# A graph layer's edge stage on one core: VectorE's rank work first in its turn, and its offset chain in two parts at other slots

## The chip, the cores and the metric

The kernel runs on one core of a Trainium2 chip. The metric is the device time in microseconds of one execution. TensorE (PE in the profile) does the matmuls, VectorE (DVE) and ScalarE (ACT) the elementwise work, GpSimd (POOL) issues the indirect transfers, and SyncE's queue (SP) the plain ones.

## What is computed

The reference is one message-passing layer with 6250 nodes and 206250 edges (100000 random pairs in both directions and a loop at each node, sorted by their destination), with a residual and a layer norm around it:

```python
row, col = src, dst
msg = concat([x[col], edge_attr], axis=1)          # 206250 x 128
h = relu(msg @ W1a.T + b1a) @ W1b.T + b1b          # 206250 x 64
sums = segment_sum(h, row, 6250); counts = segment_sum(1, row, 6250)
agg = sums / max(counts, 1)
z = relu(concat([x, agg]) @ W2a.T + b2a) @ W2b.T + b2b
out = concat([z, x]) @ Wr.T + br
y = layernorm(x + out)
```

Edges arrive sorted by `dst`, but the sums go by `src`. So each edge's result has to be moved to the place of its source node.

## The kernel before

The 206250 edges are cut into 403 quads of 512 edges. The edge stage treats two quads in each turn `m` of the table `TURNS`: quads 2m and 2m+1 enter, and the two quads before them leave. The order of every engine's work within a turn is written out by hand, one loop over `TURNS` for each engine, and the engines meet at semaphores only.

For a quad, `hidden` (L482) is the first linear layer, in float32, with a one-hot window of destination nodes that VectorE builds in `onehot` (L828). ScalarE applies the relu (L681). `message` (L492) is the second layer for two quads, into MS. ScalarE copies MS to Z (`copy_x`, L688), and beside it a class column (L692). VectorE's `rest` (L834) and `low` (L841) subtract from MS what Z holds in bfloat16, so that Z carries the float32 value in three bfloat16 parts. `permute` (L505) sorts the 512 edges of a quad by class of source node (a class is 128 nodes), with the one-hot matrices M that VectorE builds in `places` (L850) from the positions `pos`, into PA and PBk. ScalarE evicts these into stg (L703), and POOL scatters stg to the DRAM tensor `region`, at the rows that `dest` names (L1109). When all are scattered, the gather stage reads the runs of each class back, sums them by node and does the node layers.

Where an edge goes is worked out on the way. This is the rank work, in slots `i`, two for each turn:

- `rank(i)` on TensorE: class counts of a later quad into CK (L539), the rank of each edge among its class (L565, L567, into RK), and the destinations of quad i+4 (L577). `rank(2m)` stands between `hidden(2m+1)` and `permute(2m-2)`, `rank(2m+1)` at the turn's end.
- `ranks(i)` on VectorE: `positions(i+5)`, a reduction of RK to pos (L856), which must be done before TensorE's `rank(i+1)` writes RK again; in every second turn `destinations` (L926, L929); and at some slots the offset chain.

A block has 31 quads, and there are 13. When the classes of a block are counted, the offset chain works out where its edges begin in each class. It has four steps, each behind a small matmul of `rank`: `chain_copy` (L860, L864), `chain_counts` (L868 to L874), `chain_places` (L877 to L899) and `chain_steps` (L902 to L907). For block b they stand at the slots 31b-10, 31b-9, 31b-8 and 31b-7. `chain_places` copies the offsets out of RK, then does ten instructions on 50x62 values up to `dd`, which the matmul of `rank(31b-7)` reads (L560). These instructions wait for each other through the semaphore s_ch1. `stair` (L916) makes the matrix S for the destinations from them.

`classes` (L818) compares the classes of two quads `LEAD` ahead, and `index` (L797 to L809) prepares a block of indices for it, at the start of the turn. The ring OC of the comparisons holds 40 quads.

VectorE's turn before:

```python
for m in TURNS:
    # index, if a block begins at 2m+LEAD
    rest(m - 1); low(m - 1); places(2 * m - 2, 0)
    ranks(2 * m - 1)
    places(2 * m - 2, 1)
    onehot(m + 1)
    ranks(2 * m)
    stair(m + 3)
    places(2 * m - 1, 0); places(2 * m - 1, 1)
    classes(m + LEAD // 2)
```

`rest(m-1)` waits for s_x, ScalarE's class column. TensorE's `permute(2m-2, 0)` waits for s_l (`low`) and s_M (the second `places`), and `message(m)` for s_r (`rest`), since it writes MS again.

Of the kernel before, what the change touches and what calls it, by code (L numbers as in the profile page):

```python
# [38 lines left out]
LEAD = 42  # L39
# [26 lines left out]
def program(nc, xt, dstr, srcc, dstc, ea, wpk, cst, pos3, out):  # L66
# [9 lines left out]
    with ctx:  # L76
# [302 lines left out]
        def pe_ranks(i):  # L379
            return (0 <= i + 40 < NQ or 0 <= i + 5 < NQ or 0 <= i + 4 < NQ or block_at(i, 9) is not None  # L380
                    or block_at(i, 8) is not None or block_at(i, 7) is not None or i in (TABLES + 1, TABLES + 2))

        def dve_ranks(i):
            return (0 <= i + 5 < NQ or block_at(i, 10) is not None or block_at(i, 9) is not None
                    or block_at(i, 8) is not None or block_at(i, 7) is not None
                    or (0 <= i + 4 < NQ and ((i + 4) % 4 == 3 or i + 4 == NQ - 1))
                    or i in (TABLES + 1, TABLES + 2))
# [17 lines left out]
        with nc.Fori(0, trips) as _k:  # L405
            with nc.Block() as block:
# [60 lines left out]
                def _(e):  # L467
# [43 lines left out]
                    def rank(i):  # L511
# [4 lines left out]
                        b = block_at(i - 1, 10)  # L516
                        if b is not None:
                            e.wait_ge(s_ch1, LINKS * b + 2)
                        b = block_at(i - 1, 9)
                        if b is not None:  # L520
                            e.wait_ge(s_ch1, LINKS * b + 3)
                        b = block_at(i - 1, 8)
# [12 lines left out]
                        q = i + 40  # L535
# [6 lines left out]
                        b = block_at(i, 9)  # L542
# [7 lines left out]
                        b = block_at(i, 8)  # L550
# [218 lines left out]
                def _(e):  # L769
# [106 lines left out]
                    def chain_places(b):  # L876
# [3 lines left out]
                            "p (g c) -> p g c", g=2)[:, :, None, :].to_broadcast([BQ, 2, 2, CL])))  # L880
                        link(e.tensor_tensor_scan(run_in[:, :], oneg[:, :], kc[:, :], 0.0, ALU.mult, ALU.add))
# [90 lines left out]
                    def ranks(i):  # L972
                        if not dve_ranks(i):
                            return
                        e.wait_ge(s_rk, pe_count[i])
                        if 0 <= i + 5 < NQ:
                            positions(i + 5)
                        if block_at(i, 10) is not None:
                            chain_copy(block_at(i, 10))
                        if block_at(i, 9) is not None:  # L980
                            chain_counts(block_at(i, 9))
                        if block_at(i, 8) is not None:
                            chain_places(block_at(i, 8))
                        if block_at(i, 7) is not None:
                            chain_steps(block_at(i, 7))
                        if 0 <= i + 4 < NQ and ((i + 4) % 4 == 3 or i + 4 == NQ - 1):
                            destinations(i + 4)
                        if i == TABLES + 1:
                            tables()
                        if i == TABLES + 2:  # L990
                            next_pass()
# [10 lines left out]
                    for m in TURNS:  # L1002
                        for i in (2 * m + LEAD, 2 * m + LEAD + 1):
                            if i % BQ == 0 and i < NQ:
                                index(i // BQ)
                        if 0 <= m - 1 < NP:
                            rest(m - 1)
                            low(m - 1)
                            places(2 * m - 2, 0)
                        ranks(2 * m - 1)  # L1010
                        if 0 <= m - 1 < NP:
                            places(2 * m - 2, 1)
# [5 lines left out]
                        if 0 <= 2 * m - 1 < NQ:  # L1018
                            places(2 * m - 1, 0)
                            places(2 * m - 1, 1)  # L1020
                        if 0 <= m + LEAD // 2 < NP:
                            classes(m + LEAD // 2)
# [188 lines left out]
```

## Time and profile before

| | before |
|---|---|
| median of 3 runs | 1813.52 us (1808.44 to 1814.13) |
| the profiled execution | 1807.23 us, its span 1805.6 us |
| TensorE, matmuls | 1639.8 us busy, 91% |
| TensorE, weight loads | 1341.6 us, 74% |
| VectorE | 1404.7 us, 78% |
| ScalarE | 905.8 us, 50% |
| GpSimd | 1044.8 us, 58% |
| granted TensorE clock, mean | 0.963 of full |

The span is from the first to the last instruction. Up to some 55 us the kernel prepares its tables, then the edge stage runs to about 1475 us, and the rest is the gather stage. Busy shares are averages over all of these. Weight loads run beside matmuls. The number behind an instruction's name in a timeline is how many neighbouring instructions of the same kind were put in one row, and the time in brackets is how long the engine was idle before it, and for what.

### The profile page before, as it was taken

To read this page: it belongs to the slowest core of one execution; us is meant where nothing else is said; L and a number is where in the kernel's file an instruction comes from. 1 tells how busy PE (TensorE), PEld (TensorE's weight loads), DVE (VectorE), ACT (ScalarE), POOL (GpSimd) and SP (SyncE) were. 2 spreads that over 40 slices of the span, in tenths; PEclk is the share of its full clock that TensorE was granted. 3 is DMA by queue.
4 is the path that set the end of the run, shared out by engine and by line. 5 is a ranking of instruction groups with operands and counts; after the bars stand their busy time and mean duration, and the time that the engine had idled before them with its cause. 6 is when DMAs were issued, how large, how long until landed. Compare 5 with 4: busy or idle time off the path is not lost.

```text
span 1805.6 us, 40992 instructions
## 1 busy us (share of the span) xinstructions
PE 1639.8 (91%) x13455; PEld 1341.6 (74%) x13455; DVE 1404.7 (78%) x3936; ACT 905.8 (50%) x1733; POOL 1044.8 (58%) x880
## 2 busy tenths in 40 slices
PE   7899999999999999999999999999999957888787
PEld 6677777777777777777777777777777747777676
DVE  5788888888888888888888888888887745666665
ACT  2365656566565665656666565665656640011101
POOL 2376767677675776757667576775766751112210
PEclk9899999999999999999999999999999988889898
DMA  7355555555554555545555455554555658999994
GB/s 226 87 149 141 155 142 155 146 149 155 141 151 129 157 154 142 152 131 156 153 143 154 127 156 143 154 154 127 155 146 154 167 164 351 354 361 362 339 376 165
DMA packets 127789, 326.02 MB, mean 181 GB/s; under 512 B 35617, under 2 KB 68419, under 8 KB 121310
## 3 DMA queue, kind: packets, MB, share of 16 engines
q0 software_dynamic: 46080, 217.15, 37.3%
q1 hardware_dynamic: 80902, 104.09, 22.7%
q10 hardware_dynamic: 600, 2.16, 0.4%
q8 instruction: 112, 1.84, 0.4%
q14 instruction: 95, 0.78, 0.1%
HBM read 203.87 MB, written 119.40 MB: 179 GB/s over the span
## 4 chain that ended last, share of the span: by engine, by line
PE 77%; DMA 9%; DVE 7%; issue 5%; ACT 1%; POOL 0%; POOLq 0%; DVEq 0%; ACTq 0%
PE MS L492 19%; PE HH L482 19%; PE PA L505 13%; PE PBk L505 12%; DMA gbuf<-region,idx 8%; PE PA L618 5%; PE CK L539 2%; PE RK L565 2%; PE RK L567 2%; DVE OH L1032 1%; DVE M L850 1%; PE RK L577 1%; DVE Z L834 1%; DVE pos L856 0%; POOL region L1109 0%
## 5 line engine op out<-in xcount | busy, mean ns | idle before, releaser
L1109 POOL DMA_INDIRECT region<-stg,dest x806 | 968.1, 1201 | 465.9 <-ACT stg L703 283.9
L482 PE MATMUL HH<-eab,pw 128*128 128x512 f32 x806 | 438.0, 626 | 1.6 <-ACT hT L681 1.6
L850 DVE TENSOR_SCALAR M<-pos_of,pos 128x384 bf16<-128x384 int16 x1612 | 427.1, 314 | 0.1
L492 PE MATMUL MS<-W,hT 128*128 128x64 f32 x3224 | 392.7, 276 | 0.0
L492 PEld LDWEIGHTS MS<-W,hT 128*128 128x128 f32 x3224 | 382.7, 195 | 0.0
L703 ACT ACTIVATE stg<-PA 120x585 bf16<-120x585 f32 x403 | 266.4, 661 | 153.6 <-PE PA L505 153.5
L681 ACT ACTIVATE hT<-HH 128x512 f32<-128x512 f32 x403 | 240.6, 597 | 198.1 <-PE HH L482 198.1
L505 PEld LDWEIGHTS PA<-Z,M 128*128 128x128 bf16 x2418 | 215.1, 97 | 166.1 <-issue 158.0
L505 PE MATMUL PA<-Z,M 128*128 128x195 bf16 x2418 | 290.1, 255 | 38.6 <-issue 34.9
L834 DVE TENSOR_TENSOR Z<-MS,Z 128x512 f32<-128x512 f32 x202 | 139.2, 689 | 196.3 <-ACT Z L692 196.3
L505 PE MATMUL PBk<-Z,M 128*128 128x195 bf16 x2418 | 288.1, 254 | 0.0
L618 PE MATMUL PA<-gbuf,OH 128*128 128x195 bf16 x2058 | 209.9, 267 | 67.7 <-DVE OH L1032 67.6
L703 ACT ACTIVATE stg<-PBk 120x585 bf16<-120x585 f32 x403 | 265.0, 658 | 0.1
L618 PEld LDWEIGHTS PA<-gbuf,OH 128*128 128x128 bf16 x2058 | 197.7, 106 | 85.0 <-issue 80.8
L688 ACT ACTIVATE Z<-MS 128x512 f32<-128x512 f32 x202 | 120.4, 596 | 226.9 <-PE MS L492 226.9
L1032 DVE TENSOR_TENSOR OH<-laneb,ids 128x2688 bf16<-128x2688 bf16 x98 | 148.2, 1553 | 101.0 <-ACT ids L757 101.0
L505 PEld LDWEIGHTS PBk<-Z,M 128*128 128x128 bf16 x2418 | 224.5, 97 | 0.1
L1125 POOL DMA_INDIRECT gbuf<-region,idx x49 | 59.4, 1213 | 235.1 <-PE PA L618 231.4
L828 DVE TENSOR_SCALAR eab<-kb,C 64x1024 f32<-64x1024 bf16 x202 | 160.1, 793 | 6.4
L539 PEld LDWEIGHTS CK<-OC,ind 128*128 128x128 bf16 x403 | 50.5, 126 | 143.7 <-DVE pos L856 122.9
L856 DVE TENSOR_REDUCE pos<-RK 128x4 f32<-128x200 f32 x403 | 146.1, 363 | 14.1 <-PE RK L577 7.9
L841 DVE TENSOR_TENSOR Z<-Z 128x512 bf16<-128x512 f32 x202 | 150.4, 745 | 6.9
(183 smaller groups left out, 1309.3 us busy)
## 6 DMA issues: line engine op xcount, KB each, us to landing
eab<-in_ea SPq DMA_DIRECT2D x201, 256.0 KB
kb<-keyd SPq DMA_DIRECT2D x201, 128.0 KB
pw<-ptab SPq DMA_DIRECT2D x403, 32.0 KB
region<-stg,dest POOLq DMA_INDIRECT x806
ptab<-OH SPq DMA_DIRECT2D x10, 256.0 KB, 5.0
eab<-in_xt SPq DMA_DIRECT2D x12, 130.0 KB
eab<-in_xt SPq DMA_DIRECT2D x12, 128.0 KB, 8.9
out_y<-kb SPq DMA_DIRECT2D x12, 128.0 KB, 3.6
```

What stands on the lines that cost most here:

```text
L482: e.matmul(HH[:, :], pw[:, q % 4, :], eab[:, c % NB, at_q:at_q + GE], start=True, stop=True).then_inc(s_h, 1)
L492: last = e.matmul(MS[:, o:o + D], hT[:, q % 2, 128 * j:128 * j + 128], W[:, W_1B:W_1B + D], start=True, stop=True)
L505: last = e.matmul(P[:, 256 * j:256 * j + 3 * PART].rearrange("p (k f) -> p k f", k=3), M[:, q % 2, 2 * h + t, j, :], Zb[:, q // 2 % 2, :, ...
L618: last = e.matmul(o, OH[:, c % 2, k, j, :], gb[:, c % 3, ROW * k + 3 * PART * j:ROW * k + 3 * PART * (j + 1)], start=k == 0 and j == 0, st ...
L681: e.activation(hT[:, q % 2, :], HH[:, :], ACT.Relu).then_inc(s_relu, 1)
L703: e.activation(stb[:, g % NS, 0:9 * PART].rearrange("p (j f) -> p j f", j=R), P[0:KC, 0:768].rearrange("p (j f) -> p j f", j=R)[:, :, 0:3 ...
L828: e.tensor_scalar(eab[64:128, c % NB, 0:w], kb[64:128, c % NB, 0:w], C[64:128, C_P64:C_P64 + 1], None, ALU.is_equal).then_inc(s_oh, 1)
L834: e.tensor_tensor(Z[:, m % 2, 1, 0:n, 0:D], MS[:, 0:n * D].rearrange("p (j f) -> p j f", f=D), Zb[:, m % 2, 0, 0:n, 1:2 * D:2], ALU.subtra ...
L841: e.tensor_tensor(Zb[:, m % 2, 2, 0:n, 1:2 * D:2], Z[:, m % 2, 1, 0:n, 0:D], Zb[:, m % 2, 1, 0:n, 1:2 * D:2], ALU.subtract).then_inc(s_l, 1)
L850: last = e.tensor_scalar(M[:, q % 2, t, :, :], pos_of[:, :, :], pos[:, q % 16, t:t + 1], None, ALU.is_equal)
L1032: e.tensor_tensor(OH[:, c % 2, TR * h:TR * h + TR, :, :].rearrange("p k j (n u) -> p (k j) n u", u=2), lane2[:, None, :, :].to_broadcast([ ...
L1109: e.indirect_dma_start(region, bass.IndirectOffsetOnAxis(ap=dest[:, g:g + 1], axis=0), stw[:, g % NS, :], None).then_inc(s_sc[g % NS], 16)
```

## The change

`LEAD` goes from 42 to 44, and with it the counting of classes from slot i+40 to i+42. `chain_copy`, `chain_counts` and the first part of `chain_places` move to the slots 31b-12, 31b-11 and 31b-10, `chain_steps` stays at 31b-7. The ten instructions of `chain_places` after the copies become `chain_runs`, which stands behind the turn's last `places`. In VectorE's turn `ranks(2m-1)` comes first, then both halves of `places(2m-2)`, then `rest` and `low`. `index` moves from the turn's start to a place ahead of `classes`. Within `ranks`, `destinations` comes ahead of the chain.

```diff
-LEAD = 42
+LEAD = 44
...
         def pe_ranks(i):
-            return (0 <= i + 40 < NQ or 0 <= i + 5 < NQ or 0 <= i + 4 < NQ or block_at(i, 9) is not None
-                    or block_at(i, 8) is not None or block_at(i, 7) is not None or i in (TABLES + 1, TABLES + 2))
+            return (0 <= i + 42 < NQ or 0 <= i + 5 < NQ or 0 <= i + 4 < NQ or block_at(i, 11) is not None
+                    or block_at(i, 10) is not None or block_at(i, 7) is not None or i in (TABLES + 1, TABLES + 2))
...
-                        b = block_at(i - 1, 8)
+                        b = block_at(i - 1, 10)
                         if b is not None:
                             e.wait_ge(s_ch1, LINKS * b + 7)
...
-                        q = i + 40
+                        q = i + 42
                         if 0 <= q < NQ:
                             e.wait_ge(s_oc, q // 2 + 1)
...
-                        b = block_at(i, 8)
+                        b = block_at(i, 10)
                         if b is not None:
                             e.wait_ge(s_ch1, LINKS * b + 6)
...
+
+                    def chain_runs(b):
+                        after_link()
                         link(e.tensor_tensor_scan(run_in[:, :], oneg[:, :], kc[:, :], 0.0, ALU.mult, ALU.add))
...
+                        if 0 <= i + 4 < NQ and ((i + 4) % 4 == 3 or i + 4 == NQ - 1):
+                            destinations(i + 4)
+                        if block_at(i, 12) is not None:
+                            chain_copy(block_at(i, 12))
+                        if block_at(i, 11) is not None:
+                            chain_counts(block_at(i, 11))
                         if block_at(i, 10) is not None:
-                            chain_copy(block_at(i, 10))
-                        if block_at(i, 9) is not None:
-                            chain_counts(block_at(i, 9))
-                        if block_at(i, 8) is not None:
-                            chain_places(block_at(i, 8))
+                            chain_places(block_at(i, 10))
                         if block_at(i, 7) is not None:
                             chain_steps(block_at(i, 7))
-                        if 0 <= i + 4 < NQ and ((i + 4) % 4 == 3 or i + 4 == NQ - 1):
-                            destinations(i + 4)
...
                     for m in TURNS:
-                        for i in (2 * m + LEAD, 2 * m + LEAD + 1):
-                            if i % BQ == 0 and i < NQ:
-                                index(i // BQ)
+                        ranks(2 * m - 1)
                         if 0 <= m - 1 < NP:
+                            places(2 * m - 2, 0)
+                            places(2 * m - 2, 1)
                             rest(m - 1)
                             low(m - 1)
-                            places(2 * m - 2, 0)
-                        ranks(2 * m - 1)
-                        if 0 <= m - 1 < NP:
-                            places(2 * m - 2, 1)
                         if 0 <= m + 1 < NP:
                             onehot(m + 1)
                         ranks(2 * m)
...
+                        for i in (2 * m - 1, 2 * m):
+                            if block_at(i, 10) is not None:
+                                chain_runs(block_at(i, 10))
+                        for i in (2 * m + LEAD, 2 * m + LEAD + 1):
+                            if i % BQ == 0 and i < NQ:
+                                index(i // BQ)
                         if 0 <= m + LEAD // 2 < NP:
                             classes(m + LEAD // 2)
```

The first place is VectorE in a turn with destinations, in the middle of the edge stage. Z is what `rest` and `low` write, M the one-hot matrices, eab the one-hot window, S `stair`'s matrix and OC the class comparison. Before:

```order
L834 TENSOR_TENSOR Z<-MS,Z 128x8x64
L841 TENSOR_TENSOR Z<-Z 128x8x64
L850 TENSOR_SCALAR M<-pos_of,pos 128x384 x2
L856 TENSOR_REDUCE pos<-RK 128x4
L926 TENSOR_REDUCE dsum<-RK 120x8
L929 TENSOR_SCALAR dest<-dsum,C 120x8
L850 TENSOR_SCALAR M<-pos_of,pos 128x384 x2
L828 TENSOR_SCALAR eab<-kb,C 64x1024
```

Of the change:

```order
L856 TENSOR_REDUCE pos<-RK 128x4
L929 TENSOR_REDUCE dsum<-RK 120x8
L932 TENSOR_SCALAR dest<-dsum,C 120x8
L850 TENSOR_SCALAR M<-pos_of,pos 128x384 x4
L834 TENSOR_TENSOR Z<-MS,Z 128x8x64
L841 TENSOR_TENSOR Z<-Z 128x8x64
L828 TENSOR_SCALAR eab<-kb,C 64x1024
```

The instructions up to the one-hot window are the same; the reduction of RK and the destinations went from the middle to the front, and `rest` and `low` from the front to the end.

The second place is VectorE in the chain of block 5, from the last instructions of the part that makes `dd` to the steps. Before:

```order
L897 TENSOR_TENSOR dd<-dd,use 50x62
L899 TENSOR_TENSOR dd<-dd,C 50x62
L926 TENSOR_REDUCE dsum<-RK 120x8
L929 TENSOR_SCALAR dest<-dsum,C 120x8
L850 TENSOR_SCALAR M<-pos_of,pos 128x384 x2
L828 TENSOR_SCALAR eab<-kb,C 64x1024
L856 TENSOR_REDUCE pos<-RK 128x4
L902 COPY Dz<-RK 50x62
L904 TENSOR_TENSOR Dz<-Dz 50x62
```

Of the change:

```order
L900 TENSOR_TENSOR dd<-dd,use 50x62
L902 TENSOR_TENSOR dd<-dd,C 50x62
L818 TENSOR_TENSOR OC<-clsb,cls 128x400
L856 TENSOR_REDUCE pos<-RK 128x4
L929 TENSOR_REDUCE dsum<-RK 120x8
L932 TENSOR_SCALAR dest<-dsum,C 120x8
L850 TENSOR_SCALAR M<-pos_of,pos 128x384 x4
L834 TENSOR_TENSOR Z<-MS,Z 128x8x64
L841 TENSOR_TENSOR Z<-Z 128x8x64
L828 TENSOR_SCALAR eab<-kb,C 64x1024
L856 TENSOR_REDUCE pos<-RK 128x4
L905 COPY Dz<-RK 50x62
```

The part that makes `dd` now stands at the end of the turn before, behind that turn's M builds, and a whole first half of a turn lies between it and the steps.

## Rows read from the trace of the kernel before

**Rows 1.** Waits: engine line <- what it waited for: us in all, times, longest

```profile
DVE Z L834 <- ACT Z L692: 196.3, 185, 2.3
...
PE CK L539 <- DVE dsum L926: 13.1, 11, 2.3
...
PE RK L560 <- DVE dd L899: 11.9, 10, 1.8
```

**Rows 2.** One line's instructions: L692, once in each turn of the edge stage

```profile
L692 ACT ACTIVATE Z<-lid x202: 201/208/211, 63.6 to 1468.9; 128x8 f32<-128x8 f32 x101
```

**Rows 3.** Timeline, a plain turn: start, duration in us, engine, line, out<-in, count

```profile
807.12 0.20 PE L577 MATMUL RK<-Dz,S 128*128 128x3 bf16 x2
...
807.56 0.21 ACT L692 ACTIVATE Z<-lid 128x8 f32<-128x8 f32 x1
807.80 0.69 DVE L834 TENSOR_TENSOR Z<-MS,Z 128x512 f32<-128x512 f32 x1 [1.62 <-ACT Z L692]
...
808.53 0.75 DVE L841 TENSOR_TENSOR Z<-Z 128x512 bf16<-128x512 f32 x1
...
809.62 0.36 DVE L856 TENSOR_REDUCE pos<-RK 128x4 f32<-128x200 f32 x1
...
809.89 0.55 DVE L850 TENSOR_SCALAR M<-pos_of,pos 128x384 bf16<-128x384 int16 x2
...
810.37 0.20 PE L577 MATMUL RK<-Dz,S 128*128 128x3 bf16 x2
810.47 0.85 DVE L828 TENSOR_SCALAR eab<-kb,C 64x1024 f32<-64x1024 bf16 x1
...
810.54 0.72 PE L505 MATMUL PA<-Z,M 128*128 128x195 bf16 x6
...
812.08 0.99 DVE L850 TENSOR_SCALAR M<-pos_of,pos 128x384 bf16<-128x384 int16 x4
...
812.99 0.35 DVE L818 TENSOR_TENSOR OC<-clsb,cls 128x400 bf16<-128x400 bf16 x1
...
813.65 0.20 PE L577 MATMUL RK<-Dz,S 128*128 128x3 bf16 x2
```

**Rows 4.** Timeline, the turn after it, which has destinations

```profile
816.41 0.17 DVE L926 TENSOR_REDUCE dsum<-RK 120x8 f32<-120x24 f32 x1
...
816.76 0.65 DVE L850 TENSOR_SCALAR M<-pos_of,pos 128x384 bf16<-128x384 int16 x2
...
817.51 0.72 PE L505 MATMUL PA<-Z,M 128*128 128x195 bf16 x6 [0.38 <-issue]
...
820.62 0.20 PE L577 MATMUL RK<-Dz,S 128*128 128x3 bf16 x2
```

**Rows 5.** Timeline, a permute for which VectorE was not late

```profile
803.96 0.20 PE L577 MATMUL RK<-Dz,S 128*128 128x3 bf16 x2
...
804.01 0.72 PE L505 MATMUL PA<-Z,M 128*128 128x195 bf16 x6
```

**Rows 6.** Timeline, places and runs in the chain of block 5

```profile
572.26 0.20 DVE L877 COPY offs<-RK 50x62 f32<-50x62 f32 x1
...
572.85 0.27 DVE L881 TENSOR_TENSOR_SCAN run_in<-oneg,kc 50x62 f32<-50x62 f32 x1
...
574.91 0.17 DVE L926 TENSOR_REDUCE dsum<-RK 120x8 f32<-120x24 f32 x1
```

**Rows 7.** Timeline, the first instruction of index and the one that follows index

```profile
554.66 0.27 DVE L797 TENSOR_TENSOR kd<-dc,baseB 128x124 f32<-128x124 int32 x1
...
555.96 0.68 DVE L834 TENSOR_TENSOR Z<-MS,Z 128x512 f32<-128x512 f32 x1
```

**Rows 8.** Busy time by stretch: us, PE, PEld, DVE, ACT, POOL busy, clock, DMA

```profile
577.00:584.00 7.00, 7.00 (x34) 5.63 (x32) 4.69 (x16) 2.27 (x5) 2.22 (x2) 0.51 0.22 63
```

**Rows 9.** POOL's scatters: the costliest groups, then one of the timeline

```profile
L1109 POOL DMA_INDIRECT region<-stg,dest x806 | 968.1, 1201 | 465.9 <-ACT stg L703 283.9
...
812.49 1.73 POOL L1109 DMA_INDIRECT region<-stg,dest  x1 [0.30 <-issue]
```

More of the change, by code:

```diff
@@ L379, in pe_ranks @@
         def pe_ranks(i):
-            return (0 <= i + 40 < NQ or 0 <= i + 5 < NQ or 0 <= i + 4 < NQ or block_at(i, 9) is not None
-                    or block_at(i, 8) is not None or block_at(i, 7) is not None or i in (TABLES + 1, TABLES + 2))
+            return (0 <= i + 42 < NQ or 0 <= i + 5 < NQ or 0 <= i + 4 < NQ or block_at(i, 11) is not None
+                    or block_at(i, 10) is not None or block_at(i, 7) is not None or i in (TABLES + 1, TABLES + 2))
         def dve_ranks(i):
-            return (0 <= i + 5 < NQ or block_at(i, 10) is not None or block_at(i, 9) is not None
-                    or block_at(i, 8) is not None or block_at(i, 7) is not None
+            return (0 <= i + 5 < NQ or block_at(i, 12) is not None or block_at(i, 11) is not None
+                    or block_at(i, 10) is not None or block_at(i, 7) is not None
                     or (0 <= i + 4 < NQ and ((i + 4) % 4 == 3 or i + 4 == NQ - 1))
@@ L515, in rank @@
                             e.wait_ge(s_dst, i + 5)
-                        b = block_at(i - 1, 10)
+                        b = block_at(i - 1, 12)
                         if b is not None:
                             e.wait_ge(s_ch1, LINKS * b + 2)
-                        b = block_at(i - 1, 9)
+                        b = block_at(i - 1, 11)
                         if b is not None:
                             e.wait_ge(s_ch1, LINKS * b + 3)
-                        b = block_at(i - 1, 8)
+                        b = block_at(i - 1, 10)
                         if b is not None:
@@ L541, in rank @@
                                             start=k == 0, stop=k == BQ - 1)
-                        b = block_at(i, 9)
+                        b = block_at(i, 11)
                         if b is not None:
```

## The prediction

> **What bounds the kernel now.** The stretch to read is the edge stage, in which every turn treats two quads. I took the views in this order: waits, one instruction that runs once a turn, the timeline of one plain turn, one with destinations, and the turns of one offset chain.
>
> The waits show VectorE idle 196 us for ScalarE's copy of the class column (L692), and TensorE idle for two links of the rank work, at most 2.3 us at a time but only 25 us in all [rows 1]. L692 runs 202 times between 63.6 and 1468.9 us [rows 2]: 1405.3 us for 201 turns, 6.99 us a turn. About 340 us of the span lie outside (prologue and gather); the change leaves them alone.
>
> In a plain turn [rows 3] I take the end of TensorE's second rank step as T (807.12 + 0.20 = 807.32; the next is 6.53 us later). VectorE has been idle, ScalarE ends L692 at 807.77, VectorE begins `rest` at 807.80, T + 0.48, and from there works without a gap through `low`, two M builds, pos and two more M builds to 810.44, 2.64 us. TensorE's `permute(2m-2)` starts at 810.54. It needs all of that, so it starts at T + 0.48 + 2.64 + 0.10 = T + 3.22, and 3.31 us later the turn is over. The loop is closed: message, ScalarE's copy, VectorE, permute, message. That TensorE would have been ready earlier is seen where VectorE was not late: there permute starts 0.05 us after the last pair of rank matmuls has started [rows 5], here 0.17 [rows 3]. So a turn without this wait is 0.12 shorter, 6.41 us, with permute at T + 3.10.
>
> In every second turn `destinations` sits between pos and the last two M builds [rows 4]: dsum 816.41, the M builds only at 816.76 and 0.65 long, permute at 817.51, T + 3.66. This turn is 6.97 us (813.65 to 820.62).
>
> 100 plain turns of 6.53 and 101 of 6.97 make 1357 us. The other 48 us belong to the 12 chains of blocks 1 to 12, 4.0 us each (block 0's runs before the first edge).
>
> **The change part by part.** (1) *Rank work first.* `ranks(2m-1)` no longer waits behind `rest` for ScalarE; it waits only for TensorE's own rank step. I let it start 0.03 us after that step, as `rest` starts behind L692 [rows 3]: T + 0.03. What permute needs is unchanged in amount. By [rows 3], pos to M is 0.27 (809.62 to 809.89), four M builds take 0.91 up to the next start (812.08 to 812.99), `rest` 0.73, `low` 0.74: 2.65 us. `low` ends at T + 2.68. L692 (T + 0.45) has been done for a microsecond when `rest` comes (T + 1.2), so that wait is gone. Permute could start at T + 2.78; TensorE itself is ready at T + 3.10, so a plain turn is 6.41. With destinations, VectorE has 0.36 to 0.46 more (0.35 of start-to-start in [rows 4], and 0.1 of the longer M builds): permute at T + 3.15 to 3.25, so 6.46 to 6.56; I take 6.51. Saved: 100 x 0.12 + 101 x 0.46 = 58.5 us.
>
> The second half of VectorE's turn (one-hot, pos, S, four M builds, classes) is unchanged, 810.47 to 813.27, 2.8 us. VectorE is then free at T + 5.5 in a plain turn and near T + 5.95 with destinations: 0.9 and 0.55 us of slack before the next T.
>
> (2) *The chain.* Its instructions are the same. I take places as 0.59 (572.26 to 572.85), the ten instructions of `chain_runs` as 2.06 (572.85 to 574.91) [rows 6]; copy is two, counts four and steps three instructions of the size of the 0.20 row or somewhat more, with waits between: an estimate of 0.6, 0.8 and 0.7. Before, in odd blocks, all of places and runs stood between pos and M in the first half: that is TensorE's longest wait, 2.3 us [rows 1]. Now runs come after the M builds, and steps three slots later instead of one, so no TensorE matmul waits for runs directly. But 2.06 us does not fit into the slack: VectorE enters the next turn late, and what permute needs is late with it. Odd block: 2.06 less the slack of 0.9 or 0.55 is 1.2 or 1.5, and where it is 1.5 the next turn is plain and swallows 0.3: permute is 1.2 late. Even block: places and runs fall into the same second half, 2.65 less 0.9, or less 0.55 and 0.3: 1.8. The smaller pieces delay permute wherever they stand in a first half, by their length, or by 0.3 less in a plain turn. `index` (1.30 us [rows 7]), now at the turn's end, leaves VectorE 0.4 to 0.7 late into the turn of copy. So, for an odd block: runs 1.2, index and copy 1.0, places 0.5, the chain's own matmuls on TensorE 0.4 (0.3 each, one or two not hidden), 3.1 in all. For an even one: runs 1.8, index 0.4, counts 0.7, steps 0.55, matmuls 0.6, 4.05 in all. The average is 3.6 against 4.0: 5 us saved over 12 blocks.
>
> (3) *LEAD 44, slots 12, 11, 10.* One more turn in the ramp, with one class comparison of 0.35 us (L818 in [rows 3]) and 0.3 us of matmul. The waits of `classes` for the OC ring now name rank(2m), which VectorE has waited for already: nothing. Scatters get their destinations earlier: nothing, POOL isn't short of them. At the end of the stage POOL, which now has less slack a turn, may finish later than the last eviction. For ramp and end together I charge 2 us.
>
> Sum: 58.5 + 5 - 2 = 61.5, about 62 us. The profiled execution took 1807.2 us, so 1745; it is 6.3 us under the median of 1813.5, and I carry the gain over to that: **1751 us**.
>
> The ends of the unknown terms: the plain turn may stay at 6.53 (another wait at the same place), 12 us less; the turn with destinations may be 6.46 or 6.56, 5 us either way; lateness may cost 2.5 or 5 us a block, 13 less or 17 more. Together 1738 to 1765, rarely all at once.
>
> **The rivals.** *The half clock.* From 577 to 584 us the granted clock was 0.51 [rows 8], the lower of 1.2 and 2.4 GHz, right after the end of block 5's runs (574.91, [rows 6]), for which TensorE had stood idle. A stretch of some 7 us at half clock costs about 3.4. Not every odd block has such a dip, and the even blocks, whose longest wait was 1.8 us [rows 1], have none. Of my waits behind runs, the odd blocks' 1.2 to 1.5 us is under these and the even blocks' 1.8 to 2.1 between the two. If every even block falls, 6 x 3.4 = 20 us: 1771; if all twelve, 41: 1790. Against it: the waits are shorter than those that did it, and four dips of before may vanish, which are part of the 48 us above. The Trainium skill ("TensorE: Matmul & The Clock Gate", What's actually happening) has TensorE's clock set by how busy it has been; by that, a denser stage would have fewer dips, not more. The trace agrees in that its dips follow idle.
>
> *POOL becomes the bound.* A scatter takes 1.20 us on average, 0.30 between two [rows 9]: 6.0 us a turn, and the new turn is 6.46. The scatter that began at 812.49 under four M builds in a row took 1.73. Now there are two such rows of four in a turn, so a second scatter may be stretched. If two of four are (2 x 1.30 + 2 x 2.03 = 6.66 us), the pace is that of my sum, chain included (1345 us for 202 turns): no loss. At a mean of 1.70 from start to start, 6.80 a turn, the stage takes 1374 and the kernel 1782. *Its bad end is my case on the other side:* three of four stretched, 7.39 us a turn, 1493 us, 88 more than now, 1901. It decides from 1.74 us between starts (1405.3 / 202 / 4). Against it: in the turns with destinations the first row of four starts 0.4 later, beside another scatter or none. The Trainium skill ("SBUF — State Buffer", Who interferes with whom) says that a VectorE instruction in a two-port mode and GpSimd block each other wholly on a shared port; the 1.73 row fits that.
>
> *VectorE is the bound.* In 15.5 turns it has 15.5 x 5.76 + 6.0 = 95 us of 100 that TensorE now needs. If its instructions are 8% longer than I take them, through POOL, the stage loses another 25 us: 1776.
>
> *The change does not remove the wait.* If something keeps `ranks(2m-1)` waiting for a message-time event, nothing changes: 1813. TensorE's rank step ends 0.45 before L692 does [rows 3], so I see nothing that would.
>
> **How the numbers follow.** Forecast 0.66 (1738 to 1765); half clock 0.13 (1766 to 1790); POOL at its mild end or VectorE 0.13 (1766 to 1790); no gain 0.03; POOL slower than now 0.05. The range 1736 to 1788 holds the forecast and most of the next two. A measurement of this kernel can tell 0.3%, some 5 us, from no change. Faster 0.92, same 0.03, slower 0.05.
>
> **What would show it.** Right: L692's 202 runs span about 1343 us; plain turns near 6.41, the others near 6.51; no VectorE wait for L692 in most turns, but one for the last rank matmul L577; permute a tenth of a microsecond behind `low` in the turns with destinations; a permute 1.2 to 2 us late in the turn after each `chain_runs`. Wrong: plain turns of 6.53; POOL without idle time in the middle of the stage, or scatters of 1.7 us twice a turn; a granted clock of 0.5 after every block.

## The result

The change made the kernel faster by 3.5%. The chain of experiments behind it shows that most of the gain is the wait that the prediction named, and that the offset chain's part works mainly through TensorE's clock.

| | before | after |
|---|---|---|
| median of 4 runs each | 1811.54 us | 1748.69 us |
| range | 1808.44 to 1814.13 | 1745.73 to 1750.30 |
| ratio, 95% interval | | 0.9652, 0.9629 to 0.9674 |
| profiled execution | 1807.23 us, span 1805.6 | 1750.30 us, span 1748.6 |
| from first to last L692 | 1405.3 us | 1346.2 us |

1751 was predicted, with 1736 to 1788 as the range.

### The profile page after: what moved, and what is told of

Read it like the earlier page. It is cut to its first block, busy times and chain, and to the rows that moved or that the text cites. A ratio compares the mean times of both kernels' runs of the same rounds, so it can differ in the third digit from the quotient of the medians.

```text
span 1748.6 us, 40992 instructions
## 1 busy us (share of the span) xinstructions
PE 1611.3 (92%) x13455; PEld 1335.1 (76%) x13455; DVE 1411.4 (81%) x3936; ACT 906.4 (52%) x1733; POOL 1005.7 (58%) x880
## 4 chain that ended last, share of the span: by engine, by line
PE 61%; DVE 22%; DMA 9%; issue 4%; POOL 2%; ACT 1%; DVEq 0%; POOLq 0%; ACTq 0%
PE MS L492 17%; PE HH L482 12%; PE PA L505 10%; PE PBk L505 9%; DMA gbuf<-region,idx 9%; DVE M L850 6%; PE PA L618 6%; DVE Z L841 4%; DVE Z L834 3%; DVE pos L856 2%; PE RK L565 2%; PE RK L567 1%; PE CK L539 1%; POOL region L1114 1%; DVE OH L1037 1%
## 5 line engine op out<-in xcount | busy, mean ns | idle before, releaser
L1114 POOL DMA_INDIRECT region<-stg,dest x806 | 924.0, 1146 | 453.3 <-ACT stg L703 271.4
L850 DVE TENSOR_SCALAR M<-pos_of,pos 128x384 bf16<-128x384 int16 x1612 | 413.8, 315 | 0.9 <-PE PBk L505 0.4
L492 PE MATMUL MS<-W,hT 128*128 128x64 f32 x3224 | 388.1, 274 | 0.0
L492 PEld LDWEIGHTS MS<-W,hT 128*128 128x128 f32 x3224 | 378.2, 193 | 0.0
L703 ACT ACTIVATE stg<-PA 120x585 bf16<-120x585 f32 x403 | 266.6, 662 | 107.3 <-PE PA L505 106.0
L703 ACT ACTIVATE stg<-PBk 120x585 bf16<-120x585 f32 x403 | 265.2, 658 | 0.6 <-PE PBk L505 0.3
L856 DVE TENSOR_REDUCE pos<-RK 128x4 f32<-128x200 f32 x403 | 147.4, 366 | 141.2 <-PE RK L577 133.6
L1130 POOL DMA_INDIRECT gbuf<-region,idx x49 | 63.1, 1287 | 229.1 <-PE PA L618 225.3
L757 ACT ACTIVATE ids<-gbuf 128x84 bf16<-128x84 bf16 x49 | 13.7, 280 | 279.5 <-DMA gbuf<-region,idx 279.5
L828 DVE TENSOR_SCALAR eab<-kb,C 64x1024 f32<-64x1024 bf16 x202 | 151.9, 752 | 6.5
```

The lines of the kernel that those rows point to most:

```text
L492: last = e.matmul(MS[:, o:o + D], hT[:, q % 2, 128 * j:128 * j + 128], W[:, W_1B:W_1B + D], start=True, stop=True)
L703: e.activation(stb[:, g % NS, 0:9 * PART].rearrange("p (j f) -> p j f", j=R), P[0:KC, 0:768].rearrange("p (j f) -> p j f", j=R)[:, :, 0:3 ...
L850: last = e.tensor_scalar(M[:, q % 2, t, :, :], pos_of[:, :, :], pos[:, q % 16, t:t + 1], None, ALU.is_equal)
L856: e.tensor_reduce(pos[:, q % 16, :], RK[:, 0:4 * CL].rearrange("p (t c) -> p t c", t=4), AX.X, ALU.max).then_inc(s_dst, 1)
L1114: e.indirect_dma_start(region, bass.IndirectOffsetOnAxis(ap=dest[:, g:g + 1], axis=0), stw[:, g % NS, :], None).then_inc(s_sc[g % NS], 16)
```

## The profile after

Lines of the page of the kernel after: busy time, the granted clock, and three of its groups. Three lines were added to `chain_runs` and two to the loop, so L1109 is now L1114, L926 is L929 and L916 is L919; up to L880 the numbers stand.

```profile
PE 1611.3 (92%) x13455; PEld 1335.1 (76%) x13455; DVE 1411.4 (81%) x3936; ACT 906.4 (52%) x1733; POOL 1005.7 (58%) x880
...
PEclk9699999999999999999999999999999979899898
...
L1114 POOL DMA_INDIRECT region<-stg,dest x806 | 924.0, 1146 | 453.3 <-ACT stg L703 271.4
...
L856 DVE TENSOR_REDUCE pos<-RK 128x4 f32<-128x200 f32 x403 | 147.4, 366 | 141.2 <-PE RK L577 133.6
...
L834 DVE TENSOR_TENSOR Z<-MS,Z 128x512 f32<-128x512 f32 x202 | 137.0, 678 | 2.3 <-ACT Z L692 2.1
```

VectorE's wait for ScalarE's class column has gone from 196.3 us to 2.1 [rows 1]. It now waits for TensorE's rank step instead, 133.6 us at L856: that is the slack it has left. The scatters did not get longer, 1146 ns against 1201 [rows 9], and POOL is still idle for evictions.

The waits of the kernel after, TensorE's and its weight loads' (us in all, times, longest):

```profile
PEld PA L505 <- DVE Z L841: 40.2, 79, 2.1
PE PA L505 <- DVE Z L841: 28.3, 38, 2.0
```

This is `permute` waiting for `low`: the turns with destinations and those behind the chain. Now the timeline, a plain turn and the one with destinations behind it (start, duration in us, engine, line, out<-in, count, wait before):

```profile
806.35 0.20 PE L577 MATMUL RK<-Dz,S 128*128 128x3 bf16 x2
806.58 0.37 DVE L856 TENSOR_REDUCE pos<-RK 128x4 f32<-128x200 f32 x1 [0.57 <-PE RK L577]
806.78 0.21 ACT L692 ACTIVATE Z<-lid 128x8 f32<-128x8 f32 x1
806.86 1.00 DVE L850 TENSOR_SCALAR M<-pos_of,pos 128x384 bf16<-128x384 int16 x4
...
807.78 0.69 DVE L834 TENSOR_TENSOR Z<-MS,Z 128x512 f32<-128x512 f32 x1
...
808.50 0.74 DVE L841 TENSOR_TENSOR Z<-Z 128x512 bf16<-128x512 f32 x1
...
809.59 0.20 PE L577 MATMUL RK<-Dz,S 128*128 128x3 bf16 x2
809.65 0.72 PE L505 MATMUL PA<-Z,M 128*128 128x195 bf16 x6
...
812.76 0.20 PE L577 MATMUL RK<-Dz,S 128*128 128x3 bf16 x2
812.99 0.37 DVE L856 TENSOR_REDUCE pos<-RK 128x4 f32<-128x200 f32 x1 [0.91 <-PE RK L577]
...
813.62 1.19 DVE L850 TENSOR_SCALAR M<-pos_of,pos 128x384 bf16<-128x384 int16 x4
...
815.45 0.79 DVE L841 TENSOR_TENSOR Z<-Z 128x512 bf16<-128x512 f32 x1
815.99 0.20 PE L577 MATMUL RK<-Dz,S 128*128 128x3 bf16 x2
...
816.29 0.48 PEld L505 LDWEIGHTS PA<-Z,M 128*128 128x128 bf16 x6 [0.20 <-DVE Z L841]
...
819.42 0.20 PE L577 MATMUL RK<-Dz,S 128*128 128x3 bf16 x2
```

The plain turn is 6.41 us from rank step to rank step (806.35 to 812.76). `low` ends at 809.24, `permute` starts at 809.65, right behind the rank matmuls: VectorE is 0.4 us early, and TensorE has hardly a gap left. The turn with destinations is 6.66 (812.76 to 819.42). There `low` ends at 816.24 and `permute` starts 0.05 behind it. The turns with destinations alternate between 6.43 and 6.66; in the longer ones four M builds take 1.15 to 1.19 us instead of 1.00, and `low` 0.79 instead of 0.74.

The traces of before, after and of seven of the experiments were cut up in the same way, by the starts of L692. The base is the mean turn outside the chains. The excess is what the turns of a chain take above the base, summed over the blocks 1 to 12 (all in us). Where the edges of a chain are drawn moves these sums by about 1 us; the expectations have 43.6 for the change by other edges. The excess with the wait put back holds a stretch at half clock in block 4, which took 7.5 us where block 8 took 3.1.

| kernel | plain turn | with destinations | chain excess | turn 0 | L692, first to last |
|---|---|---|---|---|---|
| before | 6.52 | 6.97 | 50.4 | 6.55 | 1405.3 |
| after | 6.41 | 6.55 | 44.3 | 9.30 | 1346.2 |
| order alone | 6.41 | 6.56 | 62.5 | 9.20 | 1365.3 |
| chain alone | 6.52 | 6.97 | 34.7 | 6.56 | 1389.6 |
| with the wait put back | 6.67 | 6.88 | 36.8 | 7.49 | 1399.0 |
| runs in one piece | 6.41 | 6.56 | 73.1 | 7.49 | 1373.8 |
| destinations late | 6.41 | 6.43 | 45.4 | 7.48 | 1338.0 |
| runs in halves | 6.41 | 6.56 | 31.4 | 6.29 | 1331.3 |
| both of these | 6.41 | 6.44 | 34.9 | 9.30 | 1331.8 |

## Experiments on a chip that withholds the gain

The first four kernels were timed on another chip. There the kernel before took 1884.38 us (25 runs, 1871.83 to 1902.27), 4% more than on the first, so these four are compared with that alone.

**The change again.** No edit.

> The change itself once more, beside the pieces below. Theory (the loop through ScalarE's class column was what a turn cost): plain turns 6.41 us, turns with destinations 6.4 to 6.7, about 1749 us. It also shows whether the long half-clock stretch at the start of the edge stage (to 72.7 us; before it ended at 61.7) comes with the change or differs from run to run: if it comes with the change, the first L692 begins near 66 us and the second some 9.3 us later again.

Measured: 1899.39 us, ratio 1.0069 (1.0027 to 1.0112). The gain isn't there.

**The order alone.** The kernel before with this edit:

```diff
                     for m in TURNS:
...
+                        ranks(2 * m - 1)
                         if 0 <= m - 1 < NP:
+                            places(2 * m - 2, 0)
+                            places(2 * m - 2, 1)
                             rest(m - 1)
                             low(m - 1)
-                            places(2 * m - 2, 0)
-                        ranks(2 * m - 1)
-                        if 0 <= m - 1 < NP:
-                            places(2 * m - 2, 1)
```

> The kernel before with VectorE's turn order of the change alone; LEAD 42, the chain whole and at its old slots, destinations behind the chain in ranks. Theory (turn order carries the gain): plain turns 6.41, turns with destinations 6.55, the chains 4 to 5 us a block since all of places and runs stands before the M builds or in one second half; 1302 + 54 us for the 201 turns, about 1760 us in all, with some half-clock dips behind the odd blocks. Rival (the chain's split and new slots carry it): plain turns 6.53, about 1800.

Measured: 1919.29 us, 1.018 (1.0108 to 1.0252).

**The chain alone.** The change with the old order of VectorE's turn put back.

> The change with VectorE's old turn order (rest, low, half of the M builds, ranks, the other half); LEAD 44, split chain, new slots, index late, destinations first in ranks. Theory: plain turns stay 6.53 and turns with destinations 6.97; the runs then have some 1.05 us of VectorE's idle time before rest, so a block costs about 2.6 us instead of 4.0, and the dips behind the odd blocks go: about 1797 us. Rival (the split carries the gain): 1760.

Measured: 1874.76 us, 0.9967 (0.9932 to 1.0002).

**The change with the wait put back.**

```diff
                     for m in TURNS:
+                        if 0 <= m - 1 < NP:
+                            e.wait_ge(s_x, m)
                         ranks(2 * m - 1)
```

> The change with one wait more: VectorE waits for ScalarE's class column (s_x) at the head of the turn, ahead of ranks, as rest did before; same order otherwise. Theory (the wait's place, not the order of the instructions, is what the loop costs): plain turns 6.54, turns with destinations 6.97, chains 2.6 us a block: about 1795 us. Rival (the order of rank work ahead of TensorE's rank step matters by itself): 1749 to 1760.

Measured: 1870.76 us, 0.9928 (0.9892 to 0.9964): here the kernel with the wait that the change removed is *faster* than the change without it (1899.39).

As times, all four expectations were wrong. As ratios, the chain alone (0.992 said) and the wait put back (0.991 said) are near, and the two kernels with the new order and no wait are 4 to 5% off. The waits of the change on this chip show what is different (engine line <- releaser: us in all, times, longest):

```profile
DVE pos L856 <- remote: 136.1, 51, 5.2
ACT Z L688 <- remote: 119.1, 50, 3.0
```

There are no such rows in the trace of after. A stretch of the timeline shows one of them:

```profile
1001.03 1.91 PE L492 MATMUL MS<-W,hT 128*128 128x64 f32 x16
...
1002.25 0.66 ACT L703 ACTIVATE stg<-PBk 120x585 bf16<-120x585 f32 x1 [0.90 <-PE PBk L505]
...
1003.04 0.20 PE L577 MATMUL RK<-Dz,S 128*128 128x3 bf16 x2
...
1005.19 0.60 ACT L688 ACTIVATE Z<-MS 128x512 f32<-128x512 f32 x1 [2.28 <-remote]
1005.25 0.37 DVE L856 TENSOR_REDUCE pos<-RK 128x4 f32<-128x200 f32 x1 [2.84 <-remote]
```

and the row of that stretch in the busy times (PE, PEld, DVE, ACT, POOL busy, granted clock, share of the DMA engines, GB/s):

```profile
1001.00:1005.00 4.00, 4.00 (x37) 3.43 (x35) 1.42 (x6) 1.01 (x2) 3.02 (x3) 1.00 0.79 211
```

The message's record ends at 1002.94. ScalarE's copy of it, which waits for TensorE alone, starts at 1005.19. By the same records the copy starts 0.04 us behind the message in all 202 turns of the trace of after, and of before; on this chip it starts over a quarter of a microsecond later than that in 84 of 202, by up to 3 us. ScalarE and VectorE are let go at the same time. So TensorE's results came late there, at a granted clock that the profile gives as 1.00 (the ends of matmuls in a profile are modelled, and here that shows). Summed over the 202 copies the lateness follows the kernels' times. It is not spread evenly: in the change 121 of the 135 us fall on every second copy, the one that ends a plain turn, and so it is in the other three (125 of 153, 71 of 77, 41 of 52).

| on that chip | copies of the message late by, in all | over 1 us late | L692, first to last |
|---|---|---|---|
| order alone | 153 us | 63 | 1516.1 us |
| the change | 135 | 55 | 1495.9 |
| chain alone | 77 | 15 | 1471.7 |
| with the wait put back | 52 | 17 | 1459.6 |

I had two readings: TensorE's results come late (A), or the evictions wait for scatters to land, since stg has 8 buffers, two turns' worth, and ScalarE also waited 40.3 us at L703 for something unnamed (the ring). The second set was to tell them apart and, if it met a chip like the first, to settle the shares.

## Experiments on chips like the first

The second set of four ran on a chip where the kernel before took 1805.83 us (13 runs), the third where it took 1812.57 (13 runs). In their eight traces none of the 1616 copies of the message starts more than 0.05 us behind it.

**The order alone** (same edit).

> The kernel before with only VectorE's order changed (ranks, one-hots, add, low), the offset chain left at its old slots. It took 1919 us on a chip where the kernel before took 1884. Theory A (the gain is real where TensorE's results reach the other engines as soon as its records end, and that chip withheld them): if the kernel before takes about 1811 us here, this one takes 1752 to 1765 us and the wait of the add for ScalarE's column (196 us before) is gone; if the kernel before takes about 1884 us here, this one takes 1905 to 1930 and the copy of the message starts over 0.3 us behind the record of its matmuls in a third or more of the turns. Rival (the order alone loses on any chip, and the chain's new slots are needed for the gain): about 1.01 to 1.02 of the kernel before on either.

Measured: 1766.07 us, 0.9744 (0.9701 to 0.9787). So the order gains on this chip, 40 us, where the whole change brought 56 in the same set (the kernel with 12 buffers, below), and the rival that the order loses on any chip is out. What held the results back on the other chip this run can't tell, as it has no late copies. The order's chain excess is 62.5 us, 12 more than before. Busy time by stretch at block 5, two rows, and the timeline between them:

```profile
562.00:569.00 7.00, 5.00 (x37) 3.14 (x35) 6.56 (x27) 3.06 (x6) 3.79 (x4) 1.00 0.52 134
569.00:577.00 8.00, 7.69 (x39) 6.34 (x40) 5.79 (x19) 2.29 (x5) 2.35 (x2) 0.57 0.31 97
```

```profile
564.17 0.27 DVE L881 TENSOR_TENSOR_SCAN run_in<-oneg,kc 50x62 f32<-50x62 f32 x1
...
566.66 0.25 PE L539 MATMUL CK<-OC,ind 128*128 128x200 bf16 x1 [0.45 <-DVE dsum L926]
...
569.31 0.72 PE L505 MATMUL PA<-Z,M 128*128 128x195 bf16 x6 [1.86 <-DVE Z L841]
```

The run part of the chain (564.17 to 566.24) stands in the rank work, M, `rest` and `low` come after it, and `permute` waits 1.86 us, in a turn that had a gap of 0.45 already. TensorE's granted clock then falls from full speed (2.4 GHz) to its lower level (1.2 GHz, half) until about 577. That is so at all six odd blocks, behind waits of a permute of 1.47 to 1.86 us; in the kernel before it was four of six.

**The wait put back** (same edit).

> The change with one wait added: VectorE waits for ScalarE's column before the rank work of each turn's first slot, as the order before made it do. It took 1871 us where the kernel before took 1884. Theory A: where the kernel before takes about 1811 us, this one loses nearly all that the change gained: 1785 to 1805 us. Rival (the wait costs nothing, something else in the change gains): 1745 to 1755 us. On a chip where the kernel before takes 1884 us: 1860 to 1880 again by both.

Measured: 1803.78 us, 0.9977 (0.995 to 1.0004). One wait takes back 54 us of the change. (Its plain turn, 6.67, is longer than the 6.52 of before, so this is not exactly what the old wait cost.) Its waits have the row of before in a new place:

```profile
DVE pos L856 <- ACT Z L692: 174.3, 169, 3.2
```

**Destinations late and runs in halves together** (both edits below).

> The change with the destinations behind the 16-bit write of the message (TensorE waits for them at its second matmul group) and the runs of the chain in two halves, one slot pair earlier. Theory A: on a chip where the kernel before takes 1811 us the turns with destinations come down from 6.55 to 6.41 us (100 turns, 13 us at most) and the chain's excess of 43.6 us to about 38: 1728 to 1740 us. Rival (TensorE or the scatters bound the turn at 6.4 to 6.5 whatever VectorE does): 1745 to 1750 us. On a chip where the kernel before takes 1884 us: by theory A no gain over the change's 1899, 1880 to 1905.

Measured: 1736.08 us, 0.9601 (0.9567 to 0.9635).

**Twelve buffers for stg.** `NS = 12` instead of 8.

> The change with 12 instead of 8 buffers between ScalarE's evictions and the scatters, so that an eviction waits for the scatter of three turns ago and not of two. Ring theory (where the change does not gain, the evictions wait for scatters to land, 8 to 18 us each): on a chip where the kernel before takes 1884 us this one takes 1750 to 1800 us. Theory A (there TensorE's results come late, whatever the buffers): 1885 to 1910 us. On a chip where the kernel before takes 1811 us both say 1746 to 1751 us, no change from the 1748.7 of the change.

Measured: 1749.90 us, 0.9664 (0.9628 to 0.9699), the time of the change. So the ring costs nothing on this chip. On the other chip it wasn't tried, since the later sets did not meet it, and the ring stays untested there.

**The chain alone** (same edit).

> The change with VectorE's turn in the old order: only the chain is in two parts at its new slots, the destinations ahead of it and the index behind. The order alone brought 1766 us where the kernel before took 1806 (40 us), the whole change 57 to 63 us, so the chain's part is 17 to 23 us with the new order in place. Theory B (the chain's old slots leave TensorE without work for over 2 us in odd blocks and it then runs at half clock for about 7 us; the new slots avoid that, whatever the order): here the gain is what the four half-clock stretches of the kernel before cost, 10 to 14 us: about 0.993 of the kernel before. Rival (the chain's part only exists with the new order, where VectorE has less room): within 3 us of the kernel before. As predicted at first (chain worth 5 us by itself): 0.997. If the chip is one where the kernel before takes about 1884 us, its 0.9967 is repeated.

Measured: 1792.70 us, 0.9905 (0.9877 to 0.9933), more than I had expected. In the trace L692's span is 15.7 us shorter than before, all of it chain excess (50.4 to 34.7), with turns of 6.52 and 6.97 as before. The wait for ScalarE's column is still there, and no block has a stretch at half clock:

```profile
DVE Z L834 <- ACT Z L692: 180.1, 175, 2.1
```

In the kernel before, the odd blocks with half clock cost 6.4 us on average and the two without it 3.5, so the four dips were about 11.6 us. The other 4 are less stalling.

**The runs in one piece.** The change with the run part called right behind the placing:

```diff
                         if block_at(i, 10) is not None:
                             chain_places(block_at(i, 10))
+                            chain_runs(block_at(i, 10))
...
-                        for i in (2 * m - 1, 2 * m):
-                            if block_at(i, 10) is not None:
-                                chain_runs(block_at(i, 10))
```

> The change with the chain's run part (five operations and a scan, about 2 us) called directly behind the placing in the rank work of the slot before, and not behind the one-hots at the end of the turn. Slots and order are the change's. Theory B: a turn then holds the rank work back by some 2 us, the permutation waits for most of it, and in the odd blocks TensorE's gap may again bring half clock: 1756 to 1768 us where the change takes 1749. Rival (the new slots alone do it, since placing and steps are three slots apart now): 1748 to 1753 us.

Measured: 1773.98 us, 0.978 (0.9734 to 0.9826), above what either said. Block 3, the permute, and the two stretches around it:

```profile
351.48 0.83 PE L505 MATMUL PA<-Z,M 128*128 128x195 bf16 x4 [2.63 <-DVE Z L841]
```

```profile
345.00:352.00 7.00, 4.37 (x33) 3.01 (x33) 6.45 (x25) 3.03 (x6) 3.32 (x3) 0.94 0.43 107
352.00:360.00 8.00, 8.00 (x38) 6.53 (x37) 4.58 (x15) 2.56 (x5) 2.46 (x2) 0.50 0.25 77
```

The gap is now 2.63 us in one, and all six odd blocks lose 7.7 to 9.3 us. This kernel differs from the change only in the place of the run part, and its L692 span is 28 us longer: that the part stands behind the M builds is what matters, not the new slots. In the traces the new slots without it are even worse than the old ones with the new order (excess 73.1 against 62.5); the times of the two, 0.978 and 0.9744, don't separate them.

**Destinations late.**

```diff
                         if 0 <= i + 5 < NQ:
                             positions(i + 5)
-                        if 0 <= i + 4 < NQ and ((i + 4) % 4 == 3 or i + 4 == NQ - 1):
-                            destinations(i + 4)
...
                             rest(m - 1)
                             low(m - 1)
+                        late(2 * m - 1)
                         if 0 <= m + 1 < NP:
                             onehot(m + 1)
                         ranks(2 * m)
+                        late(2 * m)
```

`late(i)` is the two lines taken out; TensorE's wait for the destinations moves behind its count matmul (L539).

> The change with the destinations behind the 16-bit write. Both changes together (this and the halved runs) took 1736 where the change took 1750. Theory A: the turns with destinations go from 6.55 to 6.43 us, 100 times: 1736 to 1741 us. Rival (the gain of the two came from the chain): 1746 to 1750 us.

Measured: 1738.80 us, 0.9586 (0.9538 to 0.9634). The turns with destinations fell to 6.43, as expected.

**The runs in halves.** `LEAD = 46`, `OCN = 42`, copy, counts and places at the slots 14, 13 and 12; five instructions of the run part at the end of slot 12's turn, five at the end of slot 10's.

> The change with the runs of the chain in two halves and the chain's first links two slots earlier. Theory A: the chain's excess over twelve blocks falls from 43.6 to 38 to 41 us, and nothing else: 1744 to 1750 us. Rival (the gain of the two together came from the chain): 1736 to 1741 us.

Measured: 1737.86 us, 0.9597 (0.9552 to 0.9643): more than I had expected, and in the range I had given the rival. The rival's reason holds too, as the chain excess fell to 31.4 and not to 38 or 41. The longest wait of a permute for `low` is 1.3 us in it, against 2.0 in the change. Some 1.5 us of the 12.9 are block 8's stretch at half clock, which is gone. Turn 0 is 3.0 us shorter besides, and about 1 us is lost elsewhere.

The two edits don't add up. Each brings L692's span to 1338.0 and 1331.3, both to 1331.8. The turns with destinations give their 11 us in the pair as well, but it loses 3.5 in the chain, 3.0 in turn 0, and 5.1 in the turns 184 to 187, where the last block's tables stand. There the late destinations come behind the tables and `low`:

```profile
1297.16 0.25 PE L565 MATMUL RK<-OC,trib 128*128 128x200 bf16 x1 [1.58 <-DVE dsum L931]
```

```profile
1300.00:1308.00 8.00, 8.00 (x34) 6.07 (x34) 4.04 (x11) 3.03 (x6) 2.95 (x3) 0.50 0.16 47
```

Once more TensorE's gap is followed by half clock. Every run of these three is faster than every run of the change (1741.99 us at most against 1745.73 at least), and the runs don't tell the three from each other.

## Why the prediction was right, step by step

**The loop and the removed wait: right.** The plain turn was to be 6.41 and is. With destinations 6.51 was said, 6.46 to 6.56 as its bounds, and the mean is 6.55. The term was 58.5 us; it is 56.1 (0.11 us for each of 100 plain turns, 0.42 for each of 101 others, 53.6 in all, and 2.5 in the last dozen turns, which are shorter still). That it is this wait is shown from both sides: the order alone gives the turns of the change, 6.41 and 6.56, and the wait put back alone takes 54 us away and makes the turns 6.67 and 6.88. The small miss is that the M builds lengthen to 1.19 us in every other of these turns, where I had allowed 0.1.

**The chain: size nearly right, mechanism wrong.** I took 4.0 us a block before and 3.6 after, 5 us in all. The excess fell by 6.1 (50.4 to 44.3). But of the 50.4, about 11.6 were four stretches at half clock, which I had left in the 4.0 and named only among the rivals. Without them the chain took 38.8 before, and 42.8 after (44.3 less about 1.5 for one short dip: block 8 took 5.6 us, the even blocks 2, 4, 6 and 10 took 4.0 to 4.1). So the stalls grew by 4 us in the new order, and the dips' end paid for it. The estimate of the stalls was good in all: 3.1 and 4.05 us a block said for odd and even blocks, 3.3 and 4.1 measured, or 3.9 without the dip. The single waits behind the runs were less than said in the odd blocks (1.2 us said, 0.5 to 0.9 measured) and as said in the even ones (1.8; 1.5 to 2.0). And the term was mis-sized as a part of the change: with the new order in place, the new slots and the cut are worth 19 us of L692's span (1365.3 to 1346.2), since without them all six odd blocks fall to half clock.

**Ramp and end: too small.** I charged 2 us. The first L692 is 2.5 us later (66.1 for 63.6), and turn 0 takes 9.30 instead of 6.55. The reason is in the stretches at the start, before (first row) and after (second):

```profile
60.00:68.00 8.00, 7.14 (x51) 5.49 (x50) 5.04 (x13) 3.09 (x7) 0.00 (x0) 0.90 0.24 64
```

```profile
60.00:68.00 8.00, 8.00 (x30) 5.18 (x28) 2.90 (x9) 1.30 (x3) 0.00 (x0) 0.50 0.22 58
```

TensorE starts the stage at half clock, and after the change it kept it until 72.7 us, before until 61.7. Turn 0 follows the end of that stretch in the ten traces from chips like the first: 6.3 to 6.6 us where half clock ended at 61.7 to 62.8, 7.5 at 67.3 to 67.9, 9.2 to 9.3 at 71.7 to 72.7, and 10.0 at 73.8. It does not follow `LEAD` (6.55 and 9.20 with 42; 6.56, 7.5, 9.3 and 10.0 with 44; 6.29 and 9.30 with 46). Nor did it differ from run to run, which the first expectation asked: the four kernels that ran on the other chip too had nearly the same turn 0 there (the change 9.44, the order alone 9.26, the chain alone 6.56, the wait put back 7.48). What in a kernel decides it I don't know. What I had charged for is seen in the chain alone, which has the new `LEAD` and the short half clock: its first L692 is 1.0 us later than before. The other 4.2 of the 5.2 us come with the longer half clock, a term that the sum did not have. The end of the stage gave 0.4 us back.

**The sum.** 56.1 + 6.1 - 5.2 and 0.0 for the rest (tables -0.4, end +0.4) are 57.0 us, the difference of the spans (1805.6 to 1748.6); 61.5 was said. The medians differ by 62.8, as the profiled execution of before was 4 us under its median and that of after 1.6 us over. That the forecast of 1751 lies within 3 us of the measured median is therefore in part luck: on the spans the sum was 4.5 us too large.

**The rivals.** *Half clock*: as a loss it did not happen in the change. A permute waits 1.5 us in the even blocks 2, 6 and 10, 1.8 in block 12 and 2.0 in 4 and 8, and one of the six (block 8) had a dip, of 3.4 us:

```profile
871.30 1.09 PE L505 MATMUL PA<-Z,M 128*128 128x195 bf16 x6 [1.98 <-DVE Z L841]
```

```profile
871.00:875.00 4.00, 3.69 (x22) 3.52 (x22) 2.96 (x9) 1.32 (x2) 1.54 (x1) 0.57 0.48 137
```

But it was the right rival to name: it decides the kernels beside this one. One of its readings was wrong. The wait of 1.8 us in [rows 1] is not the even blocks' but that of the odd blocks 3, 7 and 11, and in 7 and 11 half clock followed; the even blocks' longest waits before were 0.9 us, and 1.1 in block 12. So waits of 1.8 us were not on the safe side. In the kernel before, block 7, its stretch behind, and block 6:

```profile
793.87 0.31 PE L560 MATMUL RK<-dd,C 50*50 50x62 f32 x2 [1.77 <-DVE dd L899]
796.00:802.00 6.00, 6.00 (x26) 4.67 (x27) 4.05 (x13) 1.58 (x4) 2.35 (x2) 0.50 0.22 64
689.44 0.25 PE L539 MATMUL CK<-OC,ind 128*128 128x200 bf16 x1 [0.94 <-DVE dsum L926]
```

*POOL*: no, its scatters take 1.15 us and it idles as before. *VectorE as the bound*: not in the plain turn, where it waits 0.57 us for TensorE; in the turns with destinations and behind the chain `permute` does wait for it, which is what the destinations late and the runs in halves won back. *The wait not removed*: no.

What I had not seen is that the gain can be away altogether on another chip. It was there in three sittings on the chip and not in the fourth. The sets of experiments ran on one chip each, so what belongs to the chip and what to the sitting is not told apart.

## What to carry over

Put first, in an in-order engine's turn, the work whose input is there, and let it cover the wait for the rest: the wait here cost 54 us, and moving three calls removed it. Then count TensorE's longest gap, not only the idle sum: side work of 2 us that stands between an input and the work that feeds TensorE costs its own length and, where half clock follows the gap, about 3 us more (here that happened behind gaps of 1.5 to 2.6 us, though not behind each of them); cut it in pieces that fit into the engine's slack behind the urgent work. And before a few per cent are believed, time the kernel before on each chip.

## What the hardware showed

- Gaps and half clock, by the longest wait of TensorE at a block. Up to 1.4 us (chain alone, runs in halves, the odd blocks of the change): no dip. 1.5 us: none of three in the change, but both in the order alone (blocks 1 and 9). 1.7 to 1.9 us: the other four odd blocks of the order alone and two of three in the kernel before, but none with the destinations late (blocks 4, 8 and 12) and none in block 12 of the change. 1.98 us: one of two in the change, both in the same kernel with 12 buffers, one of two with the wait put back. 2.3 us: two of three in the kernel before. 2.3 to 2.6 us with the runs in one piece: six of six. So the length of one gap does not decide it. A dip lasts 3.4 to 10.3 us. The Trainium skill ("TensorE: Matmul & The Clock Gate", What's actually happening) has the clock follow how busy TensorE has been. The traces agree: every dip at a block is behind a gap, and the full clock comes back in a stretch without one.
- Late results: in one sitting of four, TensorE's results came up to 3 us after their records ended in the change (up to 6 in the order alone), at a granted clock of 1.00 in the stretch shown. Whether it is TensorE itself, its reports or something else on that chip is open. The kernels with the shorter turns elsewhere had the most of it there (153 and 135 us, against 52 with the wait put back).
- Builds of M and scatters: four builds take 1.00 to 1.19 us. Of the 1612 builds of the change 104 took over 350 ns, and in 103 of these a scatter's record begins or ends; the 809 that lie wholly within a scatter's record take 307 ns on average, as do the 159 beside none. Scatters take 0.99 to 2.0 us: in the kernel before 1.29 on average beside builds and 1.00 without (1.73 in [rows 9]), in the change 1.18 and 1.10. So these rows don't bear out that builds and scatters block each other wholly, to which the prediction fitted the scatter of 1.73 us. POOL's records are rough, and a cause is not shown by this.
